# Weight folds in three groups between the first pair's products, in a one-core kernel of four attention blocks

## What is computed

```python
# block 0, 4 heads
h = batchnorm(x)
q, k, v = split(pointwise(depthwise3x3(h)));  k, v = to_7x7(k), to_7x7(v)
o = softmax((q @ k.T + rel_bias) * scale) @ v
x0 = pointwise(depthwise3x3(o)) + x
x0 = pointwise(relu(batchnorm(x0)), w_mlp) + x0
# block 1: linear attention
xn = group_norm(x0, 8)
q, k, v = xn @ qkv_w.T + qkv_b
x1 = (softmax_rows(q) @ (softmax(k).T @ v)) @ proj_w.T + proj_b + xn
# block 2: 8 heads
q, k, v = qkv_w @ group_norm(x1, 32) + qkv_b
x2 = x1 + proj_w @ (softmax(q.T @ k) @ v) + proj_b
# block 3: one head
xn = group_norm(x2, 32)
x3 = x2 + wo @ (v @ softmax(q.T @ k * c**-0.5).T) + bo
```

## Time and profile before

| | |
|---|---|
| median of 3 runs | 2170.71 us (2168.53 to 2171.08) |
| the profiled execution | 2170.37 us |
| its span, first to last instruction | 2168.3 us |
| PE busy | 2076.3 us (96%), 15232 matmuls |
| DVE busy | 1820.4 us (84%) |
| ACT busy | 1527.8 us (70%) |
| POOL busy | 1278.3 us (59%) |
| chain that ended last | PE 91%, DVE 3%, POOL 2%, the rest 4% |
| mean granted clock of PE | 0.976 |

### The profile page before, as it was taken

One profiled execution on the slowest core, in us unless ns is written; L12 is line 12 of the kernel. 1 busy time (PEld: TensorE's weight loads), 2 busy tenths in 40 slices (PEclk: granted clock), 3 DMA queues, 4 the chain that ended last, 5 costly groups with the idle time before them and its releaser, 6 DMA issues.

```text
span 2168.3 us, 58678 instructions
## 1 busy us (share of the span) xinstructions
PE 2076.3 (96%) x15232; PEld 1686.7 (78%) x15232; DVE 1820.4 (84%) x4359; ACT 1527.8 (70%) x5172; POOL 1278.3 (59%) x2954
## 2 busy tenths in 40 slices
PE   4679999999999999999999999999999999999987
PEld 3466888888888788888878888887888888788775
DVE  6778899988888998988899898888989888887532
ACT  2256777777777777777777777777777777777763
POOL 2455666666666666666666666666666666664311
PEclk8799999999999999999999999999999999999977
DMA  3000011001101100110110011011101100100000
GB/s 126 15 23 23 16 39 39 29 23 37 37 22 37 37 30 22 37 37 22 37 37 30 22 37 37 23 36 37 37 15 37 37 31 28 38 31 24 24 23 23
DMA packets 29828, 70.22 MB, mean 32 GB/s; under 512 B 6261, under 2 KB 7105, under 8 KB 29761
## 3 DMA queue, kind: packets, MB, share of 16 engines
q1 hardware_dynamic: 26928, 67.68, 9.0%
q10 hardware_dynamic: 2832, 1.73, 0.3%
HBM read 30.86 MB, written 12.85 MB: 20 GB/s over the span
## 4 chain that ended last, share of the span: by engine, by line
PE 91%; DVE 3%; POOL 2%; issue 2%; ACT 1%; SPq 1%; DMA 0%; POOLq 0%; DVEq 0%; ACTq 0%
PE ps_c L1166 19%; PE ps_a L1166 17%; PE ps_e L1166 17%; PE ps_b L1166 17%; PE ps_s L1166 10%; PE ps_s L1216 8%; POOL gn_t L579 1%; PE ps_a L1292 1%; DVE y L1158 1%; PE ps_e L1454 0%; PE ps_e L1292 0%; PE ps_b L1454 0%; PE ps_e L1399 0%; SPq L475 0%; ACT e L827 0%
## 5 line engine op out<-in xcount | busy, mean ns | idle before, releaser
L827 ACT ACTIVATE e<-ps_s,nm 98x196 f32<-98x196 f32 x1024 | 426.1, 446 | 89.9 <-DVE nm L956 89.8
L590 POOL TENSOR_SCALAR xn<-x,gn_scale,gn_shift 128x196 f32<-128x196 f32 x384 | 353.2, 933 | 20.8 <-POOL gn_shift L585 20.8
L1158 DVE SCALAR_TENSOR_TENSOR y<-opad,w_dw,y 128x406 f32<-128x406 f32 x512 | 301.8, 645 | 0.0
L1139 DVE SCALAR_TENSOR_TENSOR y<-xpad,w_dw,y 128x406 f32<-128x406 f32 x512 | 300.8, 640 | 0.0
L956 DVE TENSOR_REDUCE nm<-ps_s 98x4 f32<-98x784 f32 x256 | 240.6, 962 | 41.8 <-PE ps_s L1166 41.8
L834 ACT COPY pt<-ps_s 98x392 f32<-98x392 f32 x512 | 229.1, 503 | 42.6 <-PE ps_s L1216 41.8
L568 POOL TENSOR_TENSOR gn_t<-gn_group 128x4 f32<-128x4 f32 x96 | 34.3, 358 | 372.9 <-DVE gn_group L1006 286.5
L827 ACT ACTIVATION_READ_ACCUMULATOR e<-ps_s,nm 98x1 f32 x1024 | 231.6, 226 | 0.0
L1216 PE MATMUL ps_s<-w_eye,e 98*98 98x98 f32 x2048 | 204.6, 251 | 0.6 <-ACT e L827 0.6
L1216 PEld LDWEIGHTS ps_s<-w_eye,e 98*98 98x98 f32 x2048 | 186.3, 131 | 24.1 <-issue 16.2
L581 POOL TENSOR_SCALAR gn_t<-gn_t 128x4 f32<-128x4 f32 x288 | 119.7, 416 | 58.6 <-POOL gn_t L579 58.6
(11 more groups left out here) (245 smaller groups left out, 5596.8 us busy)
## 6 DMA issues: line engine op xcount, KB each, us to landing
...
```

Source lines behind the costliest of these rows:

```text
L590: g.tensor_scalar(dst[:, c, of_image(i)], src[:, c, of_image(i)], t.scale[:, j:j + 1], t.shift[:, j:j + 1], ALU.mult, ALU.add).then_inc(t. ...
L827: s.activation(e2[:, j, tc], tile(use)[0:HALF, of_image(tc)], ACT.Exp, bias=nm2[:, j, tc:tc + 1], accum_out=den2[:, 2 * i + tc, h:h + 1]). ...
L1139: v.scalar_tensor_tensor(out=dst, in0=window(xpad, c, k, CR), scalar=tap, in1=dst, op0=ALU.mult, op1=ALU.add).then_inc(conv1_steps.sem, 1)
L1158: v.scalar_tensor_tensor(out=dst, in0=window(opad, c, k, CR), scalar=tap, in1=dst, op0=ALU.mult, op1=ALU.add).then_inc(conv2_steps.sem, 1)
```

## The change

The folds are no longer ahead of the loop. They become three functions which PE calls within pair 0: `fold_values` (`FOLD_V1`, `FOLD_VB1`) behind the later of `q0_0`, `q0_1`; `fold_queries` (`FOLD_Q3`) behind the later of `s0_0`, `s0_1`; `fold_outputs` (the rest) behind the later of `o0_0`, `o0_1`. The splits are cut in two: `split_loaded` (ten loaded weights) stays at the old places; `split_folded` (eight folded ones and the small biases) comes on ACT behind the `o0` copies of pair 0 and on DVE ahead of the first `pw` read of pair 0. ACT's wait for `early_steps` moves ahead of the `relu` of pair 0. The copy of `heads` gets a semaphore of its own, for which `rep*` of pair 0 waits. The items are the same, but all five tables and the bank table are new.

```diff
 SP_AT = {
-    "x": -128, "res": 25, "hop": 358, "hop_out": 588, "store": 691,
+    "x": -128, "res": 204, "hop": 435, "hop_out": 665, "store": 742,
 PE_AT (from both tables)
-    "k0": 95, "s0_0": 100, "s0_1": 102, "v0": 122, "t0_1": 133, "t0_0": 134, "o0_1": 159, "o0_0": 162,
-    "pw0": 214, "pw1": 219, "kv0": 297, "hk0": 382, "hq0": 384, "sc0": 392, "hv0": 394, "sc1": 423,
-    "rep0": 537, "rep1": 539, "proj1": 544, "proj0": 550, "v3_1": 615, "v3_3": 633, "s3_0": 652, "s3_1": 657,
+    "k0": 96, "s0_0": 107, "s0_1": 110, "v0": 129, "t0_0": 143, "t0_1": 147, "o0_0": 159, "o0_1": 164,
+    "pw0": 221, "pw1": 228, "kv0": 302, "hq0": 387, "hk0": 389, "hv0": 394, "sc0": 396, "sc1": 427,
+    "rep0": 525, "rep1": 534, "proj1": 546, "proj0": 553, "v3_3": 633, "v3_1": 640, "s3_0": 657, "s3_1": 664,
...
 DVE_AT (from both tables)
-    "conv1_0": 1, "conv1_1": 3, "conv1_2": 5, "conv1_3": 33, "conv1_4": 39, "conv1_5": 42, "conv1_6": 44,
-    "conv1_7": 48, "conv1_8": 53, "s0_0": 138, "s0_1": 142, "conv2_0": 192, "conv2_1": 193, "stats1": 284,
-    "gn1": 286, "low1_0": 312, "low1_1": 318, "kv0": 328,
+    "conv1_0": 3, "conv1_1": 7, "conv1_2": 26, "conv1_3": 37, "conv1_4": 39, "conv1_5": 48, "conv1_6": 53,
+    "conv1_7": 56, "conv1_8": 58, "s0_0": 142, "s0_1": 144, "conv2_0": 193, "conv2_1": 195, "stats1": 288,
+    "gn1": 291, "low1_0": 320, "low1_1": 325, "kv0": 332,
...
 POOL_AT = {
-    "resize0": 0, "resize1": 16, "probs0": 64, "probs1": 96, "gn1": 240, "gn2": 304, "gn3": 544, "rows3": 592,
+    "resize0": 0, "resize1": 16, "probs0": 64, "probs1": 80, "gn1": 240, "gn2": 304, "gn3": 544, "rows3": 608,
...
 BANK_USES: s0_1 from "b" to "e" (beside s0_0), v0 from "b" to "a", and others
...
@@ block.scalar
+            def split_loaded():
+                act.wait_ge(weights_in, WEIGHTS)
+                for high, low, src in early_sources()[:PLAIN]:
+                    s.copy(high, src).then_inc(early_high, 1)
+            def split_folded():
+                act.wait_ge(fold_filled, FOLDS)
+                for high, low, src in early_sources()[PLAIN:]:
+                    s.copy(high, src).then_inc(early_high, 1)
+                s.copy(heads[:], w["heads"][:]).then_inc(heads_set, 1)
...
+                            if is_first(p) and use == max(("o0_0", "o0_1"), key=ACT_AT.get):
+                                split_folded()
                     for c in range(KC):
                         p = pair_of(t, u, ACT_AT[f"relu{c}"])
                         if p is not None:
+                            if is_first(p):
+                                act.wait_ge(early_steps, EARLY_STEPS)
...
@@ block.vector
+            def split_folded():
+                dve.wait_ge(early_high, PLAIN + FOLDED)
+                for high, low, src in early_sources()[PLAIN:]:
+                    v.tensor_tensor(low, src, high, ALU.subtract).then_inc(early_steps, 1)
                 dve.wait_ge(fold_filled, FOLDS)
...
                         use = f"pw{c}"
                         p = pair_of(t, u, DVE_AT[use])
                         if p is not None:
+                            if is_first(p) and use == min(("pw0", "pw1"), key=DVE_AT.get):
+                                split_folded()
...
@@ block.tensor
+                            if is_first(p) and use == latest("q0_0", "q0_1"):
+                                fold_values()
...
+                            if is_first(p) and use == latest("s0_0", "s0_1"):
+                                fold_queries()
...
+                            if is_first(p) and use == latest("o0_0", "o0_1"):
+                                fold_outputs()
```

More of the change, by code:

```diff
@@ L38 @@
 SP_AT = {
-    "x": -128, "res": 25, "hop": 358, "hop_out": 588, "store": 691,
+    "x": -128, "res": 204, "hop": 435, "hop_out": 665, "store": 742,
 }
 PE_AT = {
[9 rows of a table removed]
[9 rows of a table added]
 }
 ACT_AT = {
[11 rows of a table removed]
[11 rows of a table added]
 }
 DVE_AT = {
[10 rows of a table removed]
[10 rows of a table added]
 }
 POOL_AT = {
-    "resize0": 0, "resize1": 16, "probs0": 64, "probs1": 96, "gn1": 240, "gn2": 304, "gn3": 544, "rows3": 592,
+    "resize0": 0, "resize1": 16, "probs0": 64, "probs1": 80, "gn1": 240, "gn2": 304, "gn3": 544, "rows3": 608,
 }
 BANK_USES = {
[3 rows of a table removed]
+    "a": ("v0", "t0_0", "mlp1", "kv3", "q1_1", "hv1", "hk1", "hq1", "v3_0", "q3_1", "o3_1",),
+    "b": ("t0_1", "o0_1", "pw0", "kv0", "kv2", "q1_0", "ctx1", "out0", "hk0", "v3_2", "q3_0", "v3_1",
           "s3_1",),
[1 row of a table removed]
+    "c": ("q0_1", "q0_0", "o0_0", "pw1", "mlp0", "gn1", "gn2", "hq0", "rep0", "rep1", "proj0", "gn3",
+          "v3_3", "t3_1",),
+    "e": ("k0", "s0_0", "s0_1", "kv1", "ctx0", "out1", "hv0", "rt", "proj1", "s3_0", "t3_0", "o3_0",),
 }
@@ L442, in parts @@
                 return ws[name][:, 0, k, columns], ws[name][:, 1, k, columns], src
-            for k in range(KC):
-                yield parts("kv1", k, w["k1"][:, k])
-                for name in ("q1", "q2", "k2", "v2"):
-                    yield parts(name, k, w[name][:, k])
-            for k in range(KC):
-                yield parts("kv1", k, FOLD_V1[k], CH)
-                yield parts("q3", k, FOLD_Q3[k])
-                yield parts("v3", k, FOLD_V3[k])
-                yield parts("v3", k, FOLD_V3_KEY[k], CH)
+            loaded = [parts(name, k, w[source][:, k]) for name, source in LOADED for k in range(KC)]
+            return loaded + [entry for k in range(KC) for entry in (
+                parts("kv1", k, FOLD_V1[k], CH), parts("q3", k, FOLD_Q3[k]), parts("v3", k, FOLD_V3[k]),
+                parts("v3", k, FOLD_V3_KEY[k], CH))]
         FIRST = 16 * len(W_FIRST)
@@ L653, in _ @@
             act.wait_ge(consts_set, CONSTS)
-            def split_weights():
+            def split_loaded():
                 act.wait_ge(weights_in, WEIGHTS)
-                for n, (high, low, src) in enumerate(early_sources()):
-                    if n == PLAIN:
-                        act.wait_ge(fold_filled, FOLDS)
+                for high, low, src in early_sources()[:PLAIN]:
                     s.copy(high, src).then_inc(early_high, 1)
-                s.copy(heads[:], w["heads"][:]).then_inc(early_steps, 1)
-                act.wait_ge(early_steps, EARLY_STEPS)
+            def split_folded():
[3 more added lines that the diff above has]
+                s.copy(heads[:], w["heads"][:]).then_inc(heads_set, 1)
             def step(t):
@@ L912, in _, with split_loaded @@
             assert bn_done[0] == BN_STEPS
[L914 removed]
+            def split_loaded():
                 dve.wait_ge(weights_in, WEIGHTS)
+                for n, (high, low, src) in enumerate(early_sources()[:PLAIN]):
+                    dve.wait_ge(early_high, n + 1)
+                    v.tensor_tensor(low, src, high, ALU.subtract).then_inc(early_steps, 1)
                 v.tensor_scalar(qb2s[:], w["qb2"][:], SCALE2, None, ALU.mult).then_inc(early_steps, 1)
[L918 to L920 removed]
+            def split_folded():
+                dve.wait_ge(early_high, PLAIN + FOLDED)
+                for high, low, src in early_sources()[PLAIN:]:
                     v.tensor_tensor(low, src, high, ALU.subtract).then_inc(early_steps, 1)
@@ L1182, in _ @@
             pe.wait_ge(weights_in, WEIGHTS)
-            for m in range(KC):
-                last = product(FOLD_V1[m], lambda k: w["v1"][:, k, of_chunk(m)], lambda k: w["p1"][:, k])
-            last.then_inc(fold_filled, 1)
-            product(FOLD_VB1, lambda k: w["vb1_rep"][:, k], lambda k: w["p1"][:, k]).then_inc(fold_filled, 1)
-            for m in range(KC):
-                last = product(FOLD_Q3[m], lambda k: w["q3"][:, k, of_chunk(m)], lambda k: w["k3"][:, k])
-            last.then_inc(fold_filled, 1)
@@ L1191, in _ @@
-            for m in range(KC):
-                product(FOLD_V3[m], lambda k: w["v3"][:, k, of_chunk(m)], lambda k: w["o3"][:, k])
-                product(FOLD_V3_KEY[m], lambda k: w["q3"][:, k, of_chunk(m)],
-                        lambda k: w["kb3"][:, k:k + 1].broadcast_to([128, 2])).then_inc(fold_filled, 1)
-            for m in range(KC):
-                product(FOLD_BIAS[:, m:m + 1], lambda k: w["p2"][:, k, of_chunk(m)], lambda k: w["vb2"][:, k:k + 1])
-                product(FOLD_BIAS[:, 2 + m:3 + m], lambda k: w["k3"][:, k, of_chunk(m)], lambda k: w["qb3"][:, k:k + 1])
-                product(FOLD_BIAS[:, 4 + m:5 + m], lambda k: w["o3"][:, k, of_chunk(m)], lambda k: w["vb3"][:, k:k + 1])
@@ L1200, in _, with fold_values, fold_queries @@
-            product(FOLD_BIAS[0:HALF, 6:7], lambda k: w["qb3_rep"][:, k], lambda k: w["kb3"][:, k:k + 1]).then_inc(fold_filled, 1)
+            def fold_values():
+                for m in range(KC):
+                    last = product(FOLD_V1[m], lambda k: w["v1"][:, k, of_chunk(m)], lambda k: w["p1"][:, k])
+                last.then_inc(fold_filled, 1)
```

(15 more changed lines are left out.)

15 lines of the change are left out of this document (8 added, 7 removed), and 62 rows, old and new, of tables (ACT_AT, BANK_USES, DVE_AT, PE_AT).

## The result

The kernel after takes 2176.99 us (median of 11 runs, 2172.78 to 2179.98), the kernel before 2170.71 (11 runs, 2168.53 to 2171.38). The ratio is 1.0031, 95% interval 1.0021 to 1.0040: slower by 0.3%. The forecast was 2165.0, its range 2160 to 2175. The profiled execution of after is its slowest, 2179.98 us, span 2177.9; that of before is 2170.37, so the two profiles differ by 9.6 us where the medians differ by 6.3.

The account below looks back on a forecast made before the run. PE was taken to bound the middle, and latencies the front. Front -5.5, end -1.0 and middle +1.1 sum to -5.4 us against the profiled 2170.37, so 2165.0 us, range 2160 to 2175.

Parts of the forecast that it names:

- What bounds the kernel: PE bounds the middle (62.93 of 63.00 us busy); from 20 to 220 us a chain of latencies sets the time.
- The front, to the pw0 read: Pair 0: q products at 23.1, k0 at 33.7 behind POOL's resize, pw0 read at 64.7 against 70.11, 5.4 us earlier.
- The front, from there to stats1: pw1 and pair 1's softmax up to stats1: stats1 comes 3.5 to 6.5 us earlier, taken as 5.5.
- The rule weighed against the rows: Skill's rule: a POOL op waits one DVE instruction, 0.6 and 0.4 us; the trace rows show 6.24 and 3.67.
- Rival (4): Start of pair 0: reordered weight splits hold POOL's resize for one op only, k0 at 31.5, total 2163 us; chance 0.03.
- The later fill: DVE before out0: low1_1 behind conv2_0 and conv2_1 (about 2 us); kv0's loss is won back, nothing in sum.
- The steady state: Middle pairs: only seams between PE items count, +0.04 us per pair (-0.05 to +0.25), +1.1 us over 28.6 pairs.
- Rival (2): kv0 waits each pair because POOL's rows3 delays gn1 and low1_1; at 0.5 us per pair, 2179 us; chance 0.15.
- The end: Last pairs: proj1 can follow s3_1 directly, 1.0 us less, bounds 0 and 2.
- The sum: Whole kernel: -5.5 front, -1.0 end, +1.1 middle make -5.4 us, so 2165.0 us.

Follow-up runs that it names:

- e1: Folds in three groups and the late split, with the timetable and banks of the kernel before: 2166.88 us, ratio to before 0.9986.
- e3: The kernel after, with DVE's low1_1 between conv2_0 and conv2_1 instead of behind both: 2162.62 us, ratio 0.9968.
- e6: e3 plus one wait: in pair 0 DVE starts conv2 only after POOL's first resize op of pair 1: 2158.70 us, ratio 0.9948.
- e12: The kernel after plus only the wait that holds pair 0's conv2 until POOL's first resize op of pair 1: 2170.89 us, ratio 1.0005.

## Why the prediction was wrong

**What bounds the kernel**: right. PE is the bound in the middle, and the front's latencies are a lead for as long as nothing gives it back (e1: 3.3 us from pair 3 to the end).

**The front, to the pw0 read**: nearly right. Forecast and measured, in us: `q0` 23.1 and 23.69, `k0` 33.7 and 34.45, the first softmax add 36.8 and 38.89, `conv2` 50.2 and 52.82, `split_folded` done at 64.6 and 65.14, the `pw0` read 64.7 and 65.62. The gate of `k0` was POOL's resize, as argued. The softmax add was 2 us late since PE had idled 3.06 us ahead of `k0` and ran it and the scores at the low level (`k0` 2.00 us instead of 1.03); the estimate had taken the durations of before, where the folds ahead had kept PE busy. This differs from one execution to another: in e3, which is the same program up to there, the first folds ran at the low level (3.26 us instead of 1.89), PE idled only 0.32 us ahead of `k0`, which took 1.10 us, and `pw0` came 1.8 us earlier than in after.

**The front, from there to stats1**: wrong by 7.5 us (forecast 75, measured 82.49). The step that failed is "`pw1` stands behind `k0`: at the low level pair 1's softmax starts 5.7 us earlier". It looked at the clock and not at what `k0` of pair 1 waits for, which is POOL's resize. The prediction had the hold of POOL by back-to-back taps in its hands (3.67 us in the earlier trace rows, 6.24 in the earlier trace rows), used it for pair 0 and for the group norm, and never asked where the resize of pair 1 lies in the new order: right at `conv2`'s sixteen taps, with no pause ahead of them. With the old order of `pw1` and `k0` the hold was there too and `stats1` came at 77.32 (e1); without the hold the new order has it at 76.32 (e6). The forecast of -5.5 us for the front is nearly what is left when the two causes are taken away (e6: -4.7 at `kv0` of pair 3).

**The rule weighed against the rows**: the prediction took the rows' side, and that was right. The first op of the resize was held for 10.33 us, where the next tap's end was 0.6 us away. The Trainium skill, "SBUF — State Buffer", section "Who interferes with whom", has the op that issues second wait for the first instruction, and says that the order of issue decides who waits. Neither half is enough for these rows. The first doesn't fit 10.33 us. By the second an op that begins ahead of the run would go through, as in e6; but in after, too, the op began ahead of `conv2`, and was held. Rival (4), which rested on it, gave `k0` at 31.5: in after the op in pair 0 was held for 4.06 us and `k0` came at 34.45.

**The later fill**: wrong, and it is the step that decided, here and in the steady state. "`low1_1` now stands behind `conv2_0` and `conv2_1` on DVE (about 2 us)" was seen and priced (measured 2.4), and then closed with "what `kv0` loses is won before `out0`: nothing in sum". In the fill alone it cost 2.7 to 4.8 us at `kv0` of pair 3 (after against e3, e12 against e6).

**The steady state**: the seams were right (forecast +0.04 with bounds -0.05 and +0.25; e3 and e6, where `kv0` doesn't wait, have +0.07). If every seam cost the same, nine blocks against nine would give 0. What was missed is the wait of `kv0`, +0.39 to +0.41 us per pair. Both numbers stood in the text: 2.3 us of slack for `low1_1`, and four ops of about 2 us that the new order puts ahead of it. The first was set against POOL's `rows3` (rival 2), the second against the fill; they were never set against each other. 2.3 us of slack less 2.4 us of ops is nothing left, before any seam. This gives the sign; the 0.4 us had to be measured.

**Rival (2)**: right in its place, its sign and its size (0.5 us per pair, 2179 us; measured 0.48, 2177 us median), wrong in its mechanism, since POOL's group norm was done 7 us ahead of `low1_1`'s turn. It had a chance of 0.15. That its time came within 2 us of the median is luck: it took a front of -5.5 us and an end of -1.0, where +5.8 and -8.2 were measured. The right mechanism could have been read from the tables and one row.

**The end**: right in sign, off in size. The part that was priced, `proj1` behind `rt`, gave 0.7 us (forecast 1.0). Another 7.5 us came from stretches that the prediction didn't look at, above all from `sc1` to `sc2` (4.1 us). Which move makes them is open. By the sum of the parts the kernel would be at about 2184 us without them.

**The sum**: front and fill +5.8 instead of -5.5, middle +12.3 instead of +1.1, end -8.2 instead of -1.0. The two failed steps are of equal size, 11.3 and 11.2 us, and the end hid 7.2 of them.
